# Expert slots of a mixture-of-experts layer: small slots with the rows as the stationary operand, two low halves on GpSimd, and a later place for one weight half in big slots

## The chip, the cores and the metric

The kernel runs on one core of one Trainium2 chip. The metric is the device time in microseconds of one execution of the whole program. TensorE (PE) multiplies, VectorE (DVE), ScalarE (ACT) and GpSimd (POOL) do the elementwise work, and SyncE (SP) issues the loads and stores of this stage. The engines run side by side and wait for each other only at semaphores.

## The reference, cut to what matters

Two layers act on 4096 rows of 256 numbers. The part that the change touches is the feed-forward half of the second layer, in which each row goes to one of eight experts:

```python
gate_logits = jnp.einsum('bsd,ed->bse', x, gate_w) + gate_b + expert_bias
top_idx = jnp.argmax(gate_logits, axis=-1)
for e in range(8):
    mask = (top_idx == e)[..., None].astype(x.dtype)
    h = jax.nn.relu(jnp.einsum('bsd,df->bsf', x, w1[e]) + b1[e])   # 256 -> 1024
    y = jnp.einsum('bsf,fd->bsd', h, w2[e]) + b2[e]                # 1024 -> 256
    out = out + mask * y
```

All of it is in float32. Beside it the same rows go through four gated linear scans (the attention half of that layer), and before it stands a first layer with an attention of chunks of 32 rows and sixteen small experts.

## The kernel before, in words

**Stages.** The first half of the time is the first layer. Then the scans of the second layer begin: eight groups of 512 rows. After the first four groups the experts run, and then the other four groups and the sum of everything. This order is written out by hand for every engine; there is no planner.

**Slots.** The rows are sorted by expert (scattered to DRAM) and handled in 23 slots, one after the other. A big slot has 256 rows (two blocks), a small one 128 (one block). A round is big, big, small (k = 0, 1, 2); there are seven full rounds (`ROUND`, index r) and two big slots at the end. Each slot belongs to one expert, whose number is read from a table (`expert(n)`, a register load on SyncE), and each slot loads that expert's weights afresh: w1 (256 x 1024) and w2 (1024 x 256), 1 MB each, in halves of 512 KB.

**Split products.** To keep the accuracy of float32, each operand is split in a high part (rounded to float32r) and a low part (the rest), and each product is three matmuls: high by high, high by low, low by high (`mm3`). So for every half of a weight ScalarE writes the high part (`w1_half`, line 1405, and `w2_half`, line 1412) and VectorE subtracts to get the low part (lines 1702 and 1713), both 128 x 1024. The raw halves are single buffers: SyncE loads a half for a later slot (`raw1_half`, line 1195, `raw2_half`, line 1202) as soon as the low part of the present one is formed.

**One slot n on TensorE.** Layer 1 computes the hidden values transposed: the weights are stationary, the rows are the moving operand, 256 columns wide in a big slot and 128 in a small one; 8 blocks of 128 hidden units, 6 matmuls each, 48 in all (lines 372 to 374). They fill four PSUM banks, the quarters q = 0 to 3. Then the rows of the next slot are transposed (`rows_T`, line 1326). Layer 2 multiplies the hidden values (stationary) by w2, 256 columns wide: 48 matmuls in a big slot, 24 in a small one (lines 1360 to 1362).

**One slot on ScalarE.** The second half of w2's high part (it waits until the slot before has ended layer 2); then for each quarter a ReLU with bias (two instructions, line 1430) and a rounding (line 1436). After the second quarter stands the first half of w1 for slot n + 1, after the fourth the high part of the next rows (line 1417), w1's second half and w2's first half for slot n + 1.

**One slot on VectorE.** The same order: the result of the slot before out of PSUM with its bias (line 1728), w2's second half, the four low parts of the hidden values (line 1719) with w1's first half after the second, then the next rows' low part (line 1707), w1's second half and w2's first half.

**One slot on SyncE.** One queue, in order, and each wait holds up all behind it:

```python
store_y(...)                          # slot n - 1, waits for its result
load_b2(n)
raw2_half(n + 1, 1, e)                # waits for the low part w2, half 1, of slot n
load_rows(r, k + 2)                   # waits for the transposes of slot n + 1
load_b1(n + 1, e)                     # waits for the ReLUs of slot n
raw1_half(n + 2, 0, e)                # waits for the low part w1, half 0, of slot n + 1
raw1_half(n + 2, 1, e)
raw2_half(n + 2, 0, e)
```

**GpSimd** does nothing in the slots. The functions that the diff touches, and what calls them:

## Time and profile before

| | |
|---|---|
| median of 3 runs | 1065.47 us (1065.38 to 1067.77) |
| the profiled execution | 1066.7 us |
| its span, first to last instruction | 1064.7 us |
| mean granted TensorE clock | 0.994 |
| busy: TensorE, VectorE, ScalarE, GpSimd | 98%, 73%, 60%, 35% |
| expert slots | about 667 to 918 us of the span |

The profile is one execution. Its own time stands beside its span; the few microseconds around the span are not in the trace. Times in the rows are microseconds from the span's start. A row of a timeline gives the start, the length, the engine, the line, the operation, what it writes and reads with its shapes, and in brackets how long the engine was idle before and what ended that. Matmuls overlap in the pipeline, so what one costs is the distance from start to start and not its length.

### The profile page before, as it was taken

The numbers are of one execution on the slowest core, as the hardware profiler recorded it, in microseconds if no ns is written. First come the engines' busy times: TensorE is split into PE (matmuls) and PEld (weight loads), VectorE is DVE, ScalarE is ACT, GpSimd is POOL, SyncE is SP. The second block draws the span as 40 slices with busy tenths as digits, with TensorE's granted clock in tenths as the row PEclk, the third lists the DMA queues.
The fourth block names the chain that finished last, engine by engine and source line by source line (L and its number), as shares of the span: only waits on it lengthen the run. The fifth ranks groups of instructions, "written<-read, shape, count | busy, mean of one in ns | idle before, by whom it ended". The sixth has DMA issues, their size and how long they took to land. (4 is left out here: it accounts for less than half of the span.)

```text
span 1064.7 us, 20417 instructions
## 1 busy us (share of the span) xinstructions
PE 1039.9 (98%) x6692; PEld 933.5 (88%) x6692; DVE 773.6 (73%) x1281; ACT 638.7 (60%) x1152; POOL 373.1 (35%) x309
## 2 busy tenths in 40 slices
PE   6999999999999999999999999899999999999996
PEld 5998888989889898888877888899999999988885
DVE  5865657556575565758689889887778787588888
ACT  4554444444444444445574656789888989566664
POOL 3344443444434344453471782000000000164451
PEclk9999999999999999999999999999999999999998
DMA  5215111010111101203236366588787877332224
GB/s 178 73 56 198 41 40 59 26 73 0 39 59 39 59 0 59 79 1 139 66 115 257 109 221 233 160 250 268 241 262 241 268 247 247 126 119 99 108 70 138
DMA packets 72683, 134.73 MB, mean 127 GB/s; under 512 B 10048, under 2 KB 42688, under 8 KB 71616
## 3 DMA queue, kind: packets, MB, share of 16 engines
q1 hardware_dynamic: 63280, 120.65, 33.8%
q0 software_dynamic: 3072, 8.39, 2.4%
q10 hardware_dynamic: 6288, 5.16, 1.4%
q8 instruction: 22, 0.36, 0.1%
q14 instruction: 21, 0.17, 0.1%
HBM read 98.72 MB, written 35.45 MB: 126 GB/s over the span
## 5 line engine op out<-in xcount | busy, mean ns | idle before, releaser
L712 POOL TENSOR_TENSOR acc<-acc,ytmp 128x512 f32<-128x512 f32 x120 | 156.7, 1306 | 248.2 <-ACT ytmp L800 234.8
L1387 ACT ACTIVATE act_o<-ps,scan_bias 128x512 f32<-128x512 f32 x192 | 129.8, 688 | 103.5 <-PE ps L374 86.9
L865 DVE SCALAR_TENSOR_TENSOR hT_l<-ps,hT_h 128x512 fp32r<-128x512 f32 x128 | 87.8, 686 | 117.0 <-ACT hT_h L763 116.9
L800 ACT ACTIVATE ytmp<-ps,sel 128x256 f32<-128x256 f32 x256 | 107.6, 472 | 100.5 <-PE ps L1015 99.9
L372 PE MATMUL ps<-x1T,WB_h 128*128 128x512 f32 (+1 forms) x384 | 152.7, 398 | 2.3 <-DMA x1T<-xT_d 2.3
L374 PE MATMUL ps<-x1T,WB_l 128*128 128x512 f32 (+1 forms) x384 | 151.4, 394 | 0.0
L373 PE MATMUL ps<-x1T,WB_h 128*128 128x512 f32 (+1 forms) x384 | 150.1, 391 | 0.0
L1013 PE MATMUL ps<-vals_h,hT_h 128*128 128x256 f32 x512 | 145.2, 284 | 0.4 <-DVE hT_l L865 0.4
L1014 PE MATMUL ps<-vals_l,hT_h 128*128 128x256 f32 x512 | 143.6, 281 | 0.0
L1015 PE MATMUL ps<-vals_h,hT_l 128*128 128x256 f32 x512 | 143.4, 280 | 0.0
L763 ACT ACTIVATE hT_h<-ps 128x512 fp32r<-128x512 f32 x128 | 76.5, 598 | 99.6 <-PE ps L374 99.5
L1529 POOL DMA_INDIRECT y_b<-y_d,pos_i x20 | 25.3, 1267 | 296.9 <-DMA y_d<-y_sb 275.3
L901 DVE SCALAR_TENSOR_TENSOR acc<-ps,sel,acc 128x256 f32<-128x256 f32 x240 | 104.0, 474 | 3.0 <-PE ps L1015 2.9
L372 PE MATMUL ps<-xT_h,keys_h 128*128 128x512 f32 x256 | 104.6, 408 | 1.1 <-DVE xT_l L413 1.1
L1013 PEld LDWEIGHTS ps<-vals_h,hT_h 128*128 128x128 f32 x512 | 96.3, 188 | 8.8 <-issue 3.0
L1656 DVE TENSOR_TENSOR_SCAN h_b<-a_b,hstate,xs_b 128x512 f32<-128x512 f32 x64 | 91.7, 1433 | 16.9 <-ACT a_b L1392 11.5
L372 PE MATMUL ps<-sT_h,w_h 128*128 128x256 f32 (+1 forms) x368 | 102.4, 278 | 0.5 <-DVE w_l L1702 0.5
L374 PE MATMUL ps<-sT_h,w_l 128*128 128x256 f32 (+1 forms) x368 | 102.6, 279 | 0.0
L373 PE MATMUL ps<-sT_l,w_h 128*128 128x256 f32 (+1 forms) x368 | 102.6, 279 | 0.0
L374 PE MATMUL ps<-xT_h,keys_l 128*128 128x512 f32 x256 | 101.1, 395 | 0.0
L373 PE MATMUL ps<-xT_l,keys_h 128*128 128x512 f32 x256 | 101.0, 395 | 0.0
L1014 PEld LDWEIGHTS ps<-vals_l,hT_h 128*128 128x128 f32 x512 | 96.2, 188 | 4.4
(220 smaller groups left out, 2647.1 us busy)
## 6 DMA issues: line engine op xcount, KB each, us to landing
raw<-w SPq DMA_DIRECT2D x92, 512.0 KB, 4.9
x1T<-xT_d SPq DMA_DIRECT2D x16, 512.0 KB
comb_b<-comb_d SPq DMA_DIRECT2D x8, 1024.0 KB
xs_d<-zeros ACTq DMA_DIRECT2D x1, 4992.0 KB, 18.8
x_in<-x SPq DMA_DIRECT2D x8, 512.0 KB, 3.8
x_d<-x SPq DMA_DIRECT2D x8, 512.0 KB, 4.2
xn_d<-xn SPq DMA_DIRECT2D x8, 512.0 KB, 2.6
xT_d<-nT_h SPq DMA_DIRECT2D x8, 512.0 KB, 2.6
```

The lines of the kernel that those rows point to most:

```text
L372: pe.matmul(dst, wh, xh, start=start, stop=False)
L373: pe.matmul(dst, wh, xl, start=False, stop=False)
L374: return pe.matmul(dst, wl, xh, start=False, stop=stop)
L712: pool.tensor_tensor(dst[:, 2:4, :], acc[:, 2:4, :], ytmp[:, k % 2, :, :], ALU.add).then_inc(acc23, 1)
L800: act.activation(ytmp[:, k % 2, j - 2, :], yb(k, j), ACT.Copy, scale=sel[:, j, k:k + 1]).then_inc(y_23, 1)
L865: dve.scalar_tensor_tensor(out=hT_l[:, k % 2, :], in0=ps[:, k % 2, :], scalar=0.0, in1=hT_h[:, k % 2, :].bitcast(F32), op0=ALU.max, op1=AL ...
L901: dve.scalar_tensor_tensor(out=dst[:, j, :], in0=yb(k, j), scalar=sel[:, j, k:k + 1], in1=acc[:, j, :], op0=ALU.mult, op1=ALU.add).then_in ...
L1013: pe.matmul(yb(k, j), hT_h[:, k % 2, s], vals_h[:, k, :], start=True, stop=False)
L1014: pe.matmul(yb(k, j), hT_h[:, k % 2, s], vals_l[:, k, :], start=False, stop=False)
L1015: last_mm = pe.matmul(yb(k, j), hT_l[:, k % 2, s], vals_h[:, k, :], start=False, stop=True)
L1387: act.activation(act_o[:, i % 2, w, :], ps[:, 3 * (i % 2) + w, :], func, bias=scan_bias[:, w, i:i + 1]).then_inc(act_g, 1)
L1656: dve.tensor_tensor_scan(h_b[:, i % 2, :], a_b[:, i % 2, :], xs_b[:, i % 2, :], hstate[:, i:i + 1], ALU.mult, ALU.add).then_inc(scan_ok, 1)
```

## The change

**Small slots, TensorE.** Layer 1 has the rows stationary and the weights moving: two halves of the hidden units, 512 columns each, 6 matmuls each, into PSUM banks 0 and 1. The hidden values then stand with rows on the partitions and must be turned: eight transposes of 128 x 128 in three pieces (2, 2 and 4 of them), the transposes of the next rows between the second piece and the third.

**Small slots, the others.** VectorE adds the bias of each half (`rows_biased`, out of PSUM); the bias now lies along the free dimension, so a new buffer `b1b` of 128 x 1024 is loaded by one 512 KB broadcast instead of `b1c` (4 KB). ScalarE does one ReLU to each turned piece, which writes the high part at once (`relu_rows`), and VectorE one operation for its low part (`low_rows`). ScalarE's order is w2's second half, w1's first half of the next slot, the three ReLUs, then as before.

**GpSimd** forms two low halves in each small slot: w2's second half of this slot and w1's first half of the next. It counts on semaphores of its own.

**Big slots.** w2's second half stands after w1's first half, behind the second quarter, on ScalarE and on VectorE, and no longer ahead of the first. TensorE's wait for the ReLUs of the slot before is gone. SyncE's order stays; its waits follow the low parts, wherever they are formed (`w1_last`, `w2_last`).

```diff
+    PIECES = ((2, 0, 1), (3, 1, 1), (0, 2, 2))
...
-            def raw2_half(n, h, e):
-                if not zero(n):
-                    wait_alone(sp, w2_lo, 2 * (n - 1) + h + 1)
+            def raw2_half(r, k, h, e):
+                if not (zero(r) and k == 0):
+                    wait_alone(sp, *w2_last(r, k, h))
...
-            def load_b1(n, e):
-                if not zero(n):
-                    wait_alone(sp, t_ok, FJ * n)
+            def load_b1(r, k, e):
+                if small(k):
+                    if not zero(smalls(r, k)):
+                        wait_alone(sp, row_out, 2 * smalls(r, k))
+                    sp.dma_start(b1b[:], a["b1r"][bass.ds(e, 1)].to_broadcast((P, F1))).then_inc(b1b_in, 16)
+                    return
+                if not zero(bigs(r, k)):
+                    wait_alone(sp, t_ok, FJ * bigs(r, k))
...
+            def first_layer_rows(r, k):
+
+                for h in (0, 1):
+                    pe.wait_ge(*w1_low(r, k, h))
+                    f = slice(h * HALF1, (h + 1) * HALF1)
+                    for c in range(DC):
+                        last_mm = mm3(pe, ps[:, h, :], sT_h[:, c, 0:P], sT_l[:, c, 0:P], w1_h[:, c, f], w1_l[:, c, f],
+                                      c == 0, c == DC - 1)
+                    last_mm.then_inc(l1_full, 2)
+
+            def turn_rows(r, pieces):
+
+                for bank, q, nq in pieces:
+                    pe.wait_ge(row_out, 2 * r + 1 + q // 2)
+                    for j in range(2 * nq):
+                        f = slice((2 * q + j) * P, (2 * q + j + 1) * P)
+                        last_mm = pe.transpose(ps[:, bank, j * P:(j + 1) * P], h_rows[:, f], ident[:])
+                    last_mm.then_inc(rT_full, nq)
...
-                for q in range(FJ // 2):
-                    if not zero(n):
-                        pe.wait_ge(t_ok, FJ * (n - 1) + 2 * q + 2)
-                    elif q == 3:
+                if small(k):
+                    first_layer_rows(r, k)
+                    turn_rows(r, PIECES[0:2])
+                    rows_T(r, k + 1)
+                    turn_rows(r, PIECES[2:3])
+                for q in range(0 if small(k) else FJ // 2):
+                    if zero(n) and q == 3:
...
+            def relu_rows(r, bank, q, nq):
+                act.wait_ge(rT_full, FJ // 2 * r + q + nq)
+                act.activation(eT_h[:, 2 * q:2 * (q + nq), 0:P],
+                               ps[:, bank, 0:2 * nq * P].rearrange("p (j t) -> p j t", t=P), ACT.Relu).then_inc(e_hi, nq)
+
             def slot(r, k):
                 n, (_, st) = ROUND * r + k, blocks(r, k)
-                w2_half(n, 1)
+                if small(k):
+                    w2_half(n, 1)
+                    w1_half(n + 1, 0)
+                    for bank, q, nq in PIECES:
+                        relu_rows(r, bank, q, nq)
+                    rows_hi(r, k + 1)
+                    w1_half(n + 1, 1)
+                    w2_half(n + 1, 0)
...
                 for q in range(FJ // 2):
-                    relu(n, q, st * P)
-                    round_e(n, q, st * P)
-                    if q == 1 and left(r, k) > 0:
-                        w1_half(n + 1, 0)
+                    relu(n, bigs(r, k), q, st * P)
+                    round_e(bigs(r, k), q, st * P)
+                    if q == 1:
+                        if left(r, k) > 0:
+                            w1_half(n + 1, 0)
+                        w2_half(n, 1)
...
+            for r in range(N_SMALL):
+                n = ROUND * r + ST
+                j, f = slice(HALF2, FJ), slice(0, HALF1)
+                pool.wait_ge(w2_hi, 2 * n + 2)
+                pool.tensor_tensor(w2_l[:, j, :], raw2[:, j, :], w2_h[:, j, :].bitcast(F32), ALU.subtract).then_inc(w2_lo_p, 1)
+                pool.wait_ge(w1_hi, 2 * (n + 1) + 1)
+                pool.tensor_tensor(w1_l[:, :, f], raw1[:, :, f], w1_h[:, :, f].bitcast(F32), ALU.subtract).then_inc(w1_lo_p, 1)
...
+            def rows_biased(r, k, h):
+                n = ROUND * r + k
+                dve.wait_ge(l1_full, FJ // 2 * n + 2 * (h + 1))
+                if h == 0:
+                    dve.wait_ge(b1b_in, 16 * (smalls(r, k) + 1))
+                f = slice(h * HALF1, (h + 1) * HALF1)
+                dve.tensor_tensor(h_rows[:, f], ps[:, h, :], b1b[:, f], ALU.add).then_inc(row_out, 1)
+
+            def low_rows(r, k, bank, q, nq):
+                n = ROUND * r + k
+                dve.wait_ge(e_hi, FJ // 2 * n + q + nq)
+                j = slice(2 * q, 2 * (q + nq))
+                dve.scalar_tensor_tensor(out=eT_l[:, j, 0:P],
+                                         in0=ps[:, bank, 0:2 * nq * P].rearrange("p (j t) -> p j t", t=P),
+                                         scalar=0.0, in1=eT_h[:, j, 0:P].bitcast(F32), op0=ALU.max,
+                                         op1=ALU.subtract).then_inc(e_ok, nq)
...
-                w2_half(n, 1)
+                if small(k):
+                    rows_biased(r, k, 0)
+                    rows_biased(r, k, 1)
+                    for bank, q, nq in PIECES:
+                        low_rows(r, k, bank, q, nq)
+                    rows_lo(r, k + 1)
+                    w1_half(n + 1, 1)
+                    w2_half(n + 1, 0)
```

## Rows read from the trace of the kernel before

**Rows 1.** The page, part 1: busy time, share, count.
```profile
PE 1039.9 (98%) x6692; PEld 933.5 (88%) x6692; DVE 773.6 (73%) x1281; ACT 638.7 (60%) x1152; POOL 373.1 (35%) x309
```

**Rows 2.** Windows: one small slot, then its two big ones; busy by engine.
```profile
core 0: us, PE busy (x) PEld busy (x) DVE busy (x) ACT busy (x) POOL busy (x), PEclk, DMA share, GB/s
727.56:736.14 8.58, 8.58 (x78) 8.58 (x77) 6.13 (x10) 7.76 (x17) 0.00 (x0) 1.00 0.91 289
736.14:747.87 11.73, 11.73 (x103) 11.73 (x102) 9.92 (x12) 10.47 (x18) 0.00 (x0) 1.00 0.77 243
747.87:759.40 11.53, 11.53 (x101) 11.53 (x100) 8.62 (x11) 9.77 (x17) 0.00 (x0) 1.00 0.71 233
```

**Rows 3.** TensorE's timeline, small slot: start, length, line, operation.
```profile
...
727.56 0.22 PE L372 MATMUL ps<-sT_h,w_h 128*128 128x128 f32 x1
...
732.87 0.62 PE L1326 MATMUL ps<-ident,rows 128*128 128x128 f32 x4
...
736.14 0.28 PE L372 MATMUL ps<-sT_h,w_h 128*128 128x256 f32 x1
```

**Rows 4.** TensorE's timeline, earlier stage: 512-column matmuls, then eight transposes.
```profile
557.78 0.39 PE L373 MATMUL ps<-x1T,WB_h 128*128 128x512 f32 x1
...
560.07 0.40 PE L374 MATMUL ps<-x1T,WB_l 128*128 128x512 f32 x1
...
590.07 1.03 PE L1289 MATMUL ps<-ident,accT 128*128 128x128 f32 x8
590.87 0.47 PE L372 MATMUL ps<-x1T,WB_h 128*128 128x512 f32 x1
```

**Rows 5.** Timeline of ScalarE and of VectorE, a big slot.
```profile
749.49 0.84 ACT L1430 ACTIVATE t<-ps,b1c 128x256 f32<-128x256 f32 x2 [0.35 <-PE ps L374]
...
752.31 1.05 ACT L1405 ACTIVATE w_h<-raw 128x1024 fp32r<-128x1024 f32 x1
753.27 0.82 ACT L1430 ACTIVATE t<-ps,b1c 128x256 f32<-128x256 f32 x2
...
749.16 1.23 DVE L1713 TENSOR_TENSOR w_l<-raw,w_h 128x1024 fp32r<-128x1024 f32 x1 [0.22 <-ACT w_h L1412]
...
753.39 1.23 DVE L1702 TENSOR_TENSOR w_l<-raw,w_h 128x1024 fp32r<-128x1024 f32 x1 [0.26 <-ACT w_h L1405]
```

**Rows 6.** Timeline of ScalarE and of VectorE: tiles read from PSUM.
```profile
734.25 0.58 ACT L1417 ACTIVATE sT_h<-ps 128x512 fp32r<-128x512 f32 x1
...
756.05 0.37 ACT L1417 ACTIVATE sT_h<-ps 128x256 fp32r<-128x256 f32 x1
...
734.87 0.69 DVE L1707 TENSOR_TENSOR sT_l<-ps,sT_h 128x512 fp32r<-128x512 f32 x1
```

**Rows 7.** Timeline of SyncE's queue: when each load is issued.
```profile
755.72 0.33 SPq L1215 DMA_DIRECT2D b1c<-b  x1
757.05 2.37 SPq L1195 DMA_DIRECT2D raw<-w  x2
...
765.55 0.38 SPq L1210 DMA_DIRECT2D rows<-xs_d  x1
766.26 0.33 SPq L1215 DMA_DIRECT2D b1c<-b  x1
```

**Rows 8.** The tile raw (both weights' halves) in the slots: issue to landing.
```profile
DMA to landing us min/median/max: 4.1/4.9/5.1
```

**Rows 9.** The view of one line of GpSimd: durations least/median/most in ns, first and last start.
```profile
L719 POOL TENSOR_TENSOR xT<-xT_h,xT_l x8: 2400/2410/2851, 23.4 to 468.7; 128x1024 f32<-128x1024 f32 x8
```

**Rows 10.** GpSimd's timeline where VectorE works on two SBUF tiles.
```profile
537.47 2.21 POOL L527 TENSOR_TENSOR WB_l<-stage_b,WB_h 128x512 fp32r<-128x512 f32 x1
```

**Rows 11.** TensorE's timeline after an idle stretch, earlier stage.
```profile
562.77 0.50 PE L372 MATMUL ps<-x1T,WB_h 128*128 128x512 f32 x1 [2.30 <-DMA x1T<-xT_d]
...
564.43 0.63 PE L372 MATMUL ps<-x1T,WB_h 128*128 128x512 f32 x1
...
567.42 0.42 PE L373 MATMUL ps<-x1T,WB_h 128*128 128x512 f32 x1
```

More of the change, by code:

```diff
@@ L194, in build @@
     b2b = rc("b2b", [P, D], F32)
+    b1b = rc("b1b", [P, F1], F32)
+    h_rows = t32[:, 0:FJ // 2, :].rearrange("p j t -> p (j t)")
     w1_h = rc("w1_h", [P, DC, F1], F32R)
@@ L579, in build @@
     scat = [sem(f"scat{b}") for b in range(XN_RING)]
-    b1_in, b2_in, rows_in = (sem(n) for n in ("b1_in", "b2_in", "rows_in"))
+    b1_in, b1b_in, b2_in, rows_in = (sem(n) for n in ("b1_in", "b1b_in", "b2_in", "rows_in"))
+    row_out, rT_full = sem("row_out"), sem("rT_full")
+    w1_lo_p, w2_lo_p = sem("w1_lo_p"), sem("w2_lo_p")
     r1_in, r2_in = [sem(f"r1_in{h}") for h in (0, 1)], [sem(f"r2_in{h}") for h in (0, 1)]
@@ L605, in blocks, with bigs, smalls, small @@
         return (4 * r + ST * k, ST) if k < ST else (T // P + r, 1)
+    def bigs(r, k):
+        return ST * (r + k // ROUND) + min(k % ROUND, ST)
+    def smalls(r, k):
+        return r + k // ROUND
+    def small(k):
+        return k % ROUND == ST
+    def w1_low(r, k, h):
+        r, k = r + k // ROUND, k % ROUND
+        if k == 0 and h == 0 and not zero(r):
+            return w1_lo_p, r
+        return w1_lo, (2 * ROUND - 1) * r + 2 * k + h + 1
+    def w2_low(r, k, h):
+        r, k = r + k // ROUND, k % ROUND
+        if small(k) and h == 1:
+            return w2_lo_p, r + 1
+        return w2_lo, (2 * ROUND - 1) * r + 2 * k + h + 1
+    def w1_last(r, k, h):
+        r, k = r + k // ROUND, k % ROUND
+        return w1_low(r, k - 1, h) if k else (w1_lo, (2 * ROUND - 1) * r + h)
+    def w2_last(r, k, h):
+        r, k = r + k // ROUND, k % ROUND
+        if k:
+            return w2_low(r, k - 1, h)
+        return (w2_lo_p, r) if h else (w2_lo, (2 * ROUND - 1) * r)
+    PIECES = ((2, 0, 1), (3, 1, 1), (0, 2, 2))
     def every_slot(slot, eng):
@@ L1196, in raw1_half @@
                              a["w1"][bass.ds(e, 1), h].rearrange("a p c f -> p (a c) f")).then_inc(r1_in[h], 16)
-            def raw2_half(n, h, e):
-                if not zero(n):
-                    wait_alone(sp, w2_lo, 2 * (n - 1) + h + 1)
+            def raw2_half(r, k, h, e):
+                if not (zero(r) and k == 0):
+                    wait_alone(sp, *w2_last(r, k, h))
                 j = slice(h * HALF2, (h + 1) * HALF2)
@@ L1347, in slot @@
                     last_mm.then_inc(l1_full, 1)
-                if left(r, k) > 0:
+                if left(r, k) > 0 and not small(k):
                     rows_T(r, k + 1)
@@ L1449, in slot @@
                     w2_half(n + 1, 0)
-                if zero(r) and k == 2:
-                    mixture_sigmoids(act, mix2, 2)
                 if left(r, k) == 1:
@@ L1744, in slot @@
                     rows_out(*((r, k - 1) if k else (r - 1, ROUND - 1)))
-                w2_half(n, 1)
+                if small(k):
[6 more added lines that the diff above has]
+                    w2_half(n + 1, 0)
+                    if zero(r):
+                        mixture_pieces(k)
+                    return
                 for q in range(FJ // 2):
                     low_e(n, q, st * P)
-                    if q == 1 and left(r, k) > 0:
-                        w1_half(n + 1, 0)
+                    if q == 1:
+                        if left(r, k) > 0:
+                            w1_half(n + 1, 0)
+                        w2_half(n, 1)
                 if left(r, k) > 0:
```

47 lines of the change are left out of this document (25 added, 22 removed).

## The prediction

> **What bounds the kernel now.** I read the page's busy shares first, then the windows of one round, then the timelines of the engines in it. TensorE is busy for 98% of the span [rows 1]. The change lies in the 23 expert slots. One small slot and its two big ones last 8.58, 11.73 and 11.53 us, TensorE is busy in all of it at the full clock, and no other engine is [rows 2]. So this stage is TensorE's: what it saves there counts, as long as nobody makes it wait. The reader is to see two more things in the windows: ScalarE is busy 7.76 of the 8.58 us of a small slot, and the DMA share there is already 0.91, at 289 GB/s [rows 2].
>
> All sums are made against the profiled execution, 1066.7 us (span 1064.7). The median of the three runs is 1065.47, 1.2 us lower; I take 1.2 off at the end. I count 0.3%, 3.2 us, as about what a measurement of this kernel tells from no change.
>
> **TensorE's own sum, per small slot.** Layer 1 with the weights stationary is 48 matmuls of 128 columns, 727.56 to 732.87: 5.31 us, 0.111 each [rows 3]. The rest, 732.87 to 736.14, is four transposes of the next rows and 24 matmuls of 256 columns: 3.27 us [rows 3]. With rows stationary, layer 1 is 12 matmuls of 512 columns. Ten such starts took 557.78 to 560.07, 0.229 each [rows 4]: 12 cost 2.75 us. Eight transposes of 128x128 are added, and eight took 590.07 to 590.87, 0.80 us [rows 4]. So 5.31 goes, 3.55 comes: 1.76 less per small slot, 12.3 for seven. With no wait at all the slot is 6.82 us and the profiled time 1054.4.
>
> **The chain inside the small slot.** Layer 1's sum now passes VectorE (bias), TensorE (transposes), ScalarE (ReLU) and VectorE (low part) before layer 2. Count from the slot's start. Layer 1 ends at 2.75; a handoff to another engine costs about 0.2 (in a big slot 12 of 96 matmuls, 11.3 us by rows 2, end at 1.42, and ScalarE's ReLU starts at 749.49, 1.62 after 747.87 [rows 2, 5]). The bias on 128x512 is a PSUM read of 0.69 [rows 6], to 3.6; the last four transposes end at about 4.1; ReLU on 128x512, 0.58, and the low part, 0.69 [rows 6], end at about 5.6. Layer 2's first half runs until then, and its second half, 1.44, ends at 7.0 to 7.1. So the chain's floor is 7.1, not 6.82: 1.5 less than now, 10.4 us in all. ScalarE and VectorE lose work in this slot (eight ReLUs and four roundings become three ReLUs; two low parts go to GpSimd), so their busy time is no bound.
>
> **GpSimd's two low halves.** A two-input operation on 128x1024 took 2.41 us there [rows 9] against VectorE's 1.23 [rows 5]. The first starts when ScalarE has rounded the second half of weight 2, near 2.4 (below), and ends at 4.8; layer 2 wants it at about 5.6 or later. The second follows ScalarE's rounding of the next slot's weight 1, first half. Both are covered, at a cost of nothing, if GpSimd isn't slowed; a rival has the price of the lost cover.
>
> **The moved step, and SyncE's queue.** This is where I part from the full gain. In a big slot ScalarE rounded the second half of weight 2 first, and VectorE's low part ended at 749.16 + 1.23 = 750.39, 2.52 into the slot [rows 5]. Now both come after the second quarter and after weight 1's first half. ScalarE takes that half at 752.31, 4.44 in, 0.96 each [rows 5], so the moved rounding is 5.40 to 6.4. VectorE takes the weight 1 part at 753.39, 5.52 in, 1.23 long [rows 5], and ends the moved part near 7.95 (twice 1.23, less a little overlap). For layer 2 of the same slot that is in time: its last 24 matmuls begin 2.8 before the end, at 8.7. The later two ReLU quarters are 0.96 later; the third's low part ends near 8.5, against 8.7: a cover of only 0.2, which I cost at nothing (losing it costs what it overshoots, in 16 slots).
>
> But SyncE's queue is in order, and its next load, raw2's second half for the next slot, waits for that low part. Behind it stand the rows load, the new b1b load, then raw1's first half for the slot after. Issues without a wait stand 0.71 apart, 1.33 where an expert number is read first [rows 7]. From 7.95: rows 8.66, b1b 9.37, raw1 first half 10.70. Before, that raw1 load was issued at 757.05, 9.18 in [rows 2, 7]. It is 1.5 later. And ahead of it in 2.75 us go 512 + 256 + 512 KB, where b1c was a few KB.
>
> Who waits? In the small slot ScalarE's order is: second half of weight 2, then the first half of weight 1 that this load brings, and only then the three ReLUs. Its wait holds back the ReLUs, and so layer 2. With L from issue to landing, and the big slot 11.53 long [rows 2], it lands L - 0.83 into the small slot. Then 0.96 rounding, 0.42 ReLU of a 128x256 piece (0.37 [rows 6] and a bit), about 0.45 for its low part (0.69 [rows 6], scaled by ScalarE's 0.37/0.58), and 24 matmuls, 2.87. The slot is L + 3.9. It equals today's 8.58 at L = 4.7. GpSimd's second part ends 2.4 after the rounding, before the slot does.
>
> L is 4.1 least, 4.9 median, 5.1 most in this stage today [rows 8]. Lower bound 4.1: slot 8.0, 4.1 us saved in all. Upper bound: 289 GB/s at share 0.91 is 318 GB/s flat out [rows 2], so 1.31 MB needs 4.1 us where 2.75 have passed; 4.9 + 1.35 = 6.25, slot 10.15, 11 us lost. The nearest row is the 5.1 of a half queued behind others, so I take 5.2: slot 9.1, +0.5 in each of seven, +3.6. b1b, issued 1.33 earlier, holds the bias back to about 3 and TensorE's turning with it, but that wait lies under ScalarE's and adds nothing. Sum: 1066.7 + 3.6 - 1.2 = 1069.1.
>
> The Trainium skill's page DMA: Bandwidth & Descriptors, section Anatomy of one DMA — SWDGE (gpsimd) path, fits 2.0 us plus bytes over 436 GB/s to each transfer of that path; by it a half of 512 KB would take an estimated 3.2 us, the wait would go, and the second rival below would come true. The trace disagrees: no half landed under 4.1.
>
> **Other edits.** ScalarE's first work in a big slot is gone, which gives nothing since the ReLU waits for TensorE at 1.62 anyway [rows 5]. TensorE's wait for the ReLUs of the slot before never bound. The 512 KB b1b load seven times is counted above. Everything ahead of the slots and after them is unchanged.
>
> **Rivals.**
> 1. Forecast: raw1's first half is late, L 4.1 to 6.25, 1061 to 1076, likeliest 1069. For it: the queue order and rows 7 and 8. Against: only half a microsecond from balance.
> 2. Faster: the load is in time (L under 3.8, or SyncE issues earlier than I reckon, with ScalarE free by 3.5 of the slot). Then b1b is next: landing near 3, bias 3.7 and 4.4, four transposes, ReLU and low part to 6.1, slot 7.1 to 7.6, 1054 to 1060. For it: ScalarE has over 1.7 us less work. It decides below L = 4.2.
> 3. The clock. After 2.30 idle seven 512-column matmuls took 564.43 to 567.42, 0.427 each instead of 0.229 [rows 4, 11]: the 1.2 GHz level instead of 2.4, at 1.4 us more. My small slot has 2.2 us of idle, in two pieces. If a fall comes each time, seven times 1.4 more: 1079. One or two falls are inside the forecast.
> 4. GpSimd is slowed. Its 128x512 operation took 2.21 beside VectorE's two-input work [rows 10] instead of 1.2 (half of 2.41). At 4.4 for a half, weight 1's low part comes 9.6 into the slot, past its end of 9.1: 4 us more, 1073. Against: VectorE's work in that stretch reads PSUM. Beside this stands the Trainium skill, SBUF — State Buffer, section Who interferes with whom: a VectorE instruction with two SBUF inputs and a GpSimd one that reads SBUF exclude each other, one with a PSUM input does not. The 2.21 agrees; by the rule only the two weight parts at the slot's end can collide.
>
> **Chances.** Rival 1 0.63 (slower 0.31, same 0.24, faster 0.08), rival 2 0.18 (0.16 faster, 0.02 same), rival 3 0.11, rival 4 0.08, both slower. Slower 0.50, same 0.26, faster 0.24. The likeliest gives 1069.0; its own range is 1062 to 1075. For 8 in 10 over all I take 1058.5 to 1075.5: it leaves out the best of rival 2 and most of rival 3.
>
> **What would show it.** Right: L1405's successor waiting 2 us and more for the raw DMA in small slots; TensorE idle before layer 2 there; small slots near 9; SyncE waiting 3 us for VectorE's moved part; 512-column matmuls 0.229 apart; big slots still 11.5 to 11.7. Wrong: small slots of 7 to 8 us without a DMA wait; clock below 1.00 in most rounds; TensorE waiting for GpSimd's part; big slots longer.

## The result and the profile after

The changed kernel takes 1084.61 us (median of four runs, 1084.39 to 1086.36) where the kernel before takes 1065.97 (four runs, 1065.38 to 1067.77): the ratio is 1.0177, 95% interval 1.0165 to 1.0189. It is 18.6 us slower. The forecast was 3.6 us slower, 1069.1, with 1075.5 as the upper end of its range. The profiled execution of the changed kernel took 1084.73, with a span of 1082.9.

The page shows TensorE with less work (1034.8 us busy instead of 1039.9) and a smaller share, 96% where [rows 1] have 98%:

```profile
PE 1034.8 (96%) x6496; PEld 920.3 (85%) x6496; DVE 765.4 (71%) x1274; ACT 617.9 (57%) x1089; POOL 407.2 (38%) x323
```

I measured each slot from its first layer-1 matmul to that of the next slot. The whole loss lies there: the 23 slots take 269.1 us instead of 251.0, 18.1 more. In order, a semicolon after each round, the changed kernel's slots are 17.42, 11.55, 12.70; 11.78, 11.64, 10.88; 11.72, 11.63, 10.42; 11.73, 11.63, 10.50; 11.72, 11.63, 10.31; 11.73, 11.62, 10.96; 11.72, 11.63, 11.05; 11.75, 11.36. Before they were 16.91, 11.50, 8.58, and then 11.73, 11.50, 8.58 six times. So the seven small slots cost 16.8 us more, the second big slots 0.8, and the first slot 0.5. Windows over one round (two big slots, then the small one), to lay beside [rows 2]:

```profile
core 0: us, PE busy (x) PEld busy (x) DVE busy (x) ACT busy (x) POOL busy (x), PEclk, DMA share, GB/s
743.44:755.16 11.72, 11.72 (x103) 11.72 (x101) 8.08 (x11) 9.79 (x17) 0.00 (x0) 1.00 0.64 213
755.16:766.79 11.63, 11.63 (x100) 11.57 (x99) 8.59 (x11) 9.68 (x18) 0.00 (x0) 1.00 0.73 232
766.79:777.21 10.42, 7.39 (x50) 6.27 (x49) 6.43 (x11) 5.67 (x8) 4.77 (x2) 1.00 0.92 318
```

In the small slot TensorE is busy 7.39 of 10.42 us; in [rows 2] it was busy in all of 8.58. Its own timeline says where it stands idle (compare [rows 3]):

```profile
766.79 0.39 PE L374 MATMUL ps<-w_h,sT_h 128*128 128x512 f32 x1
...
769.36 0.39 PE L376 MATMUL ps<-w_h,sT_l 128*128 128x512 f32 x1
771.69 0.66 PE L1395 MATMUL ps<-ident,t 128*128 128x128 f32 x4 [1.94 <-DVE t L1821]
772.18 0.60 PE L1375 MATMUL ps<-ident,rows 128*128 128x128 f32 x4
772.62 0.60 PE L1395 MATMUL ps<-ident,t 128*128 128x128 f32 x4
774.30 0.39 PE L1431 MATMUL ps<-w_h,eT_h 128*128 128x256 f32 x1 [1.09 <-DVE eT_l L1827]
...
777.21 0.28 PE L374 MATMUL ps<-sT_h,w_h 128*128 128x256 f32 x1
```

Layer 1 is as short as reckoned: twelve matmuls from 766.79 to 769.36 and one pitch, 0.233 each, 2.8 us. Then come two waits: 1.94 us for the bias add (L1821) before the hidden values are turned (L1395, the transposes), and 1.09 for the ReLU's low part (L1827) before layer 2 (L1431). ScalarE shows what stands behind the second:

```profile
766.99 1.07 ACT L1483 ACTIVATE w_h<-raw 128x1024 fp32r<-128x1024 f32 x1 [0.33 <-PE ps L1433]
772.46 1.06 ACT L1476 ACTIVATE w_h<-raw 128x1024 fp32r<-128x1024 f32 x1 [4.40 <-DMA raw<-w]
773.43 1.12 ACT L1511 ACTIVATE eT_h<-ps 128x256 fp32r<-128x256 f32 x3
```

It waits 4.40 us for raw1's first half, with the three ReLUs queued behind. The view of waits over the stage counts it (what waited, for whom, us in total, times, longest):

```profile
ACT w_h L1476 <- DMA raw<-w: 30.5, 7, 4.6
...
PE ps L1395 <- DVE t L1821: 16.1, 7, 3.9
DVE t L1821 <- DMA b1b<-b1r: 14.0, 6, 2.6
```

SyncE's queue in the same round, to lay beside [rows 7]:

```profile
763.44 0.34 SPq L1246 DMA_DIRECT2D raw<-w  x1
764.27 0.38 SPq L1254 DMA_DIRECT2D rows<-xs_d  x1
764.91 0.33 SPq L1260 DMA_DIRECT2D b1b<-b1r  x1
766.23 1.53 SPq L1239 DMA_DIRECT2D raw<-w  x2
```

raw1's first half is issued 11.07 us into the big slot (766.23 less 755.16) and ScalarE starts on it 6.23 later. I call this time L. In the six later rounds it is 6.46, 6.23, 6.26, 6.11, 6.24 and 6.37. The prediction's L ends at the landing, for which it took 5.2; the traces give no landing for this half in the changed kernel, and where they give one (x13, the later rounds) ScalarE starts 0.1 after it.

### The profile page after: what moved, and what is told of

Read it like the earlier page. It is cut to its first block and busy times, and to the rows that moved or that the text cites. A ratio compares the mean times of both kernels' runs of the same rounds, so it can differ in the third digit from the quotient of the medians.

```text
span 1082.9 us, 19855 instructions
## 1 busy us (share of the span) xinstructions
PE 1034.8 (96%) x6496; PEld 920.3 (85%) x6496; DVE 765.4 (71%) x1274; ACT 617.9 (57%) x1089; POOL 407.2 (38%) x323
## 5 line engine op out<-in xcount | busy, mean ns | idle before, releaser
L1749 DVE TENSOR_TENSOR_SCAN h_b<-a_b,hstate,xs_b 128x512 f32<-128x512 f32 x64 | 92.2, 1440 | 16.8 <-ACT a_b L1463 11.4
L1431 PE MATMUL ps<-w_h,eT_h 128*128 128x256 f32 x312 | 90.9, 291 | 6.6 <-DVE eT_l L1827 4.5
L1059 PEld LDWEIGHTS ps<-vals_h,hT_l 128*128 128x128 f32 x512 | 96.8, 189 | 0.0
L1645 POOL TENSOR_TENSOR w_l<-raw,w_h 128x1024 fp32r<-128x1024 f32 x7 | 16.6, 2374 | 210.1 <-ACT w_h L1483 210.1
L1432 PE MATMUL ps<-w_l,eT_h 128*128 128x256 f32 x312 | 87.4, 280 | 0.0
```

What stands on the lines that cost most here:

```text
L1059: last_mm = pe.matmul(yb(k, j), hT_l[:, k % 2, s], vals_h[:, k, :], start=False, stop=True)
L1431: pe.matmul(dst, eT_h[:, j, t], w2_h[:, j, :], start=j == 0, stop=False)
L1749: dve.tensor_tensor_scan(h_b[:, i % 2, :], a_b[:, i % 2, :], xs_b[:, i % 2, :], hstate[:, i:i + 1], ALU.mult, ALU.add).then_inc(scan_ok, 1)
```

## The experiments

Theories. Q: the moved rounding holds SyncE's queue, and that is the loss. B: the new bias load, 512 KB in the queue ahead of raw1's first half, is slow itself and delays what stands behind it. Against them: ScalarE's order in the small slot, GpSimd's part, the clock, and theory M, the first round's gate pieces on VectorE (`mixture_pieces`: small operations on 128x32 and less that rank the rows' gate values; they run only in the first round). Every ratio is to the kernel before, run on the same chip beside it. A slot's time is read from one profiled execution of each kernel.

| kernel | edit | median us | ratio, 95% interval |
|---|---|---|---|
| x1 | changed, move undone | 1065.7 | 0.9993 (0.9978 to 1.0009) |
| x2 | before, move alone | 1074.1 | 1.0075 (1.0058 to 1.0092) |
| x3 | changed, b1b loaded once | 1077.5 | 1.0098 (1.0081 to 1.0115) |
| x4 | changed, raw1's half issued first | 1078.9 | 1.0134 (1.0089 to 1.0178) |
| x5 | x1, gate pieces after the small slot | 1067.0 | 0.9998 (0.9984 to 1.0013) |
| x6 | x1, other queue order | 1065.1 | 0.9989 (0.9973 to 1.0005) |
| x7 | x5 and x6 | 1063.6 | 0.9965 (0.9952 to 0.9978) |
| x8 | changed, other queue order, move kept | 1072.5 | 1.0052 (1.0034 to 1.0070) |
| x9 | x6, gate pieces in the first slot | 1061.8 | 0.9949 (0.9933 to 0.9966) |
| x10 | x1, GpSimd's halves on VectorE | 1067.4 | 1.0005 (0.9994 to 1.0016) |
| x11 | changed, ReLUs first | 1086.4 | 1.0181 (1.0155 to 1.0208) |
| x12 | before, GpSimd's halves alone | 1073.1 | 1.0058 (1.0037 to 1.0080) |
| x13 | changed, biases stored 128 times | 1081.8 | 1.0147 (1.0125 to 1.0169) |
| x14 | changed, b1b into one partition | 1079.2 | 1.0111 (1.0092 to 1.0129) |

### x1: the move undone

```diff
+                w2_half(n, 1)
                 for q in range(FJ // 2):
 ...
-                    if q == 1:
-                        if left(r, k) > 0:
-                            w1_half(n + 1, 0)
-                        w2_half(n, 1)
+                    if q == 1 and left(r, k) > 0:
+                        w1_half(n + 1, 0)
```

The same on ScalarE and on VectorE, in big slots only.

> The changed kernel, with the second half of weight 2 again first in big slots. Theory Q, the moved half holds back SyncE's queue and that is the whole loss: raw1's first half is issued 1.5 us earlier and lands in 5.2, small slots fall from 10.7 to 8.2 or less, time about 1067. Theory B, the 512 KB bias load is itself slow and holds up raw1's first half behind it in the queue: the half is issued 1.3 us earlier but still takes 6.2 us to land, small slots 9.3 to 9.4, time 1074 to 1076. If neither the queue nor the load sets the small slot (the new chain through VectorE and TensorE costs it), nothing changes: 1084.

Measured 1065.7, near Q's 1067 and 9 us under B's 1074 to 1076: all of the loss goes. In the profile a big slot starts at 755.15, the small one behind it at 766.65. SyncE's queue, then ScalarE:

```profile
762.15 0.33 SPq L1260 DMA_DIRECT2D b1b<-b1r  x1
763.47 3.35 SPq L1239 DMA_DIRECT2D raw<-w  x2
```

```profile
769.50 1.07 ACT L1476 ACTIVATE w_h<-raw 128x1024 fp32r<-128x1024 f32 x1 [1.59 <-DMA raw<-w]
```

raw1's first half is issued 8.32 us in, 2.75 earlier than in the changed kernel; I had reckoned with 1.3. The kernel before issued it at 9.18 because b1c ahead of it waits for the slot's last ReLUs [rows 7]; b1b waits for nothing recent. L is still 6.03. With the half 2.75 earlier ScalarE waits only 1.59, and after the first round small slots are 7.53 to 8.02. So Q names the edit that costs, while B's slow load is there too and is now nearly hidden. The profile is of one of the two executions of ten that took 1071.5 (the others took 1063.5 to 1067.1), and its first round is long: 18.30 in its first big slot and 14.35 in its small one, at a granted clock of 0.81 and 0.76.

### x2: the move alone, in the kernel before

```diff
-                w2_half(n, 1)
+                if small(k):
+                    w2_half(n, 1)
                 for q in range(FJ // 2):
 ...
                     if q == 1 and left(r, k) > 0:
                         w1_half(n + 1, 0)
+                    if q == 1 and not small(k):
+                        w2_half(n, 1)
```

> The kernel before, with only the move of weight 2's second half in big slots. Theory Q at full strength: raw1's first half is 1.5 us later and small slots grow by about that, 1076. Theory B: behind it there is no bias load of 512 KB, it lands in 5.1, near 4.2 into the small slot, and ScalarE, which does two ReLU quarters ahead of it, comes to it at about 3.5: small slots 0 to 0.7 longer, 1066 to 1071.

Measured 1074.1, 8 us more than before, over B's 1066 to 1071 and under Q's 1076. The mechanism is neither as I wrote it: small slots stay at 8.58 to 8.84, and it is the big slot behind them that grows, from 11.73 to between 12.11 and 12.99. ScalarE there:

```profile
773.47 0.84 ACT L1434 ACTIVATE t<-ps,b1c 128x256 f32<-128x256 f32 x2 [2.21 <-DMA b1c<-b]
```

Its first ReLU waits for b1c, a load of 4 KB that stands behind the halves and the rows. The waits of this stage hold that wait six times, 10.1 us; the kernel before has none. SyncE's row for that load:

```profile
768.98 0.33 SPq L1219 DMA_DIRECT2D b1c<-b  x1
```

It is issued 6.90 into the small slot (which starts at 762.08), as before (766.26 less 759.37, 6.89 [rows 7]). So it isn't issued late but lands late: ScalarE starts on it 4.5 after its issue, where before 3.4 (766.26 to 769.65) was enough. What differs ahead of it is the queue. The move keeps SyncE still until 8 to 9 us into the big slot and then lets five loads (raw2's second half, the rows, and the three halves for the slot after) go in a bunch. That b1c pays for this bunch fits the rows; no run separates it.

### x3, x14, x13: what b1b costs the load behind it

```diff
# x3: only the first round's load is left, and VectorE waits for that one
+                if small(k) and not zero(smalls(r, k)):
+                    return
                 if small(k):
-                    if not zero(smalls(r, k)):
-                        wait_alone(sp, row_out, 2 * smalls(r, k))
...
# x14: later loads go to one partition, 4 KB
-                    sp.dma_start(b1b[:], a["b1r"][bass.ds(e, 1)].to_broadcast((P, F1)))...
+                    p = P if zero(smalls(r, k)) else 1
+                    sp.dma_start(b1b[0:p, :], a["b1r"][bass.ds(e, 1)].to_broadcast((p, F1)))...
# x13: 512 KB as before, but 128 different rows
-                    sp.dma_start(b1b[:], a["b1r"][bass.ds(e, 1)].to_broadcast((P, F1)))...
+                    sp.dma_start(b1b[:], a["b1r"][bass.ds(e, 1)].rearrange("a p f -> (a p) f"))...
...
-        "b1r": c(i["L1_ffn_b1"]),
+        "b1r": c(np.repeat(i["L1_ffn_b1"][:, None, :], P, axis=1)),
```

> The changed kernel with the bias load b1b only ahead of the first small slot; the later small slots use that one's bias, so their rows are those of another expert's bias. Theory B: raw1's first half is issued 0.65 us earlier and lands in 5.2 instead of 6.2 to 6.5, small slots about 8.7 to 8.9, time 1071 to 1073. Theory Q alone: only the 0.65 of the issue comes back, small slots about 10.0, time 1080.

> The changed kernel, b1b loaded whole ahead of the first small slot and later into one partition only (4 KB; the other 127 keep the first one's bias). Issue, order and wait stay, the 512 KB go. If b1b's transfer is what costs (R or its bytes): raw1's first half lands 4.1 after its issue at 11.0, small slots 8.3 to 9, and as in x3 the slot behind them waits for b1c: 1076 to 1079. If the issue and its place cost: 1084.

> The changed kernel with the biases stored 128 times over in the chip's memory, so that b1b is still 512 KB to 128 partitions, but no two of them read the same row. In the changed kernel raw1's first half lands 6.2 after its issue behind b1b, in x3, with no b1b, 4.1, and while b1b moves the DMA engines carry 189 GB/s instead of 400. Theory R, the one row read 128 times is slow: b1b then moves at 400 GB/s, 1.3 us, raw1's first half lands in 5.2 to 5.4, small slots 9.7 to 9.9, time 1077 to 1080. Theory P, it is the place or the bytes of any such load: 6.2 stays, and 1084.

L of the six later rounds, from SyncE's issue to ScalarE's start:

| kernel | L of each round | mean |
|---|---|---|
| changed | 6.46 6.23 6.26 6.11 6.24 6.37 | 6.3 |
| x13, 128 rows | 5.29 5.96 5.57 5.22 5.59 6.17 | 5.6 |
| x3, no b1b | 4.71 4.06 3.88 5.05 4.82 3.91 | 4.4 |
| x14, 4 KB | 5.13 3.66 3.84 4.82 3.98 3.78 | 4.2 |

One pair of rows for L in x3 (issue, then ScalarE's start):

```profile
765.70 2.12 SPq L1239 DMA_DIRECT2D raw<-w  x2
```

```profile
769.76 1.07 ACT L1476 ACTIVATE w_h<-raw 128x1024 fp32r<-128x1024 f32 x1 [1.61 <-DMA raw<-w]
```

So b1b's issue and its place cost nothing measurable in L (x14 against x3; they cost 0.6 to 0.7 by making raw1's issue later, 11.1 to 11.2 into the slot against 10.5). 512 KB of different rows cost 1.4 us of L (x13 against x14), and that the 128 partitions read one row costs 0.65 more (6.28 less 5.63). b1b's own landing shows the cost of the one row directly, 0.9; first the changed kernel, then x13:

```profile
DMA to landing us min/median/max: 5.5/6.0/6.2
```

```profile
DMA to landing us min/median/max: 5.0/5.1/5.3
```

Windows over the stretch in which b1b moves and, for the changed kernel, the one behind it agree; first the changed kernel, then x13:

```profile
766.50:770.00 3.50, 3.25 (x16) 2.36 (x15) 2.20 (x3) 1.23 (x2) 1.86 (x1) 1.00 0.76 189
770.00:773.00 3.00, 1.31 (x12) 1.29 (x12) 1.29 (x2) 0.54 (x1) 0.52 (x1) 1.00 1.03 400
```

```profile
766.50:770.00 3.50, 3.33 (x17) 2.43 (x15) 2.28 (x3) 1.31 (x2) 1.79 (x1) 1.00 0.92 304
```

With one row the DMA engines carry 189 GB/s, with 128 rows 304. Theory B holds in this size. But the gains in time are small, 3 us in x13, 5 in x14, 7 in x3, and the times miss what I expected: x13's 1081.8 lies between R's 1077 to 1080 and P's 1084, and x3's 1077.5 is over B's 1071 to 1073. In x3 and x14 a part is given back. x3's small slots fall to between 7.53 and 8.68 after the first round, and the big slots behind them, 11.73 in the kernel before, take 12.25 to 14.13, where ScalarE waits for b1c as in x2:

```profile
778.76 0.47 ACT L1501 ACTIVATE t<-ps,b1c 128x256 f32<-128x256 f32 x1 [2.53 <-DMA b1c<-b]
```

### x4 and x8: another order in SyncE's queue, the move kept

```diff
# x4, in SyncE's slot; and not again further down where k == 1
+                if k == 1 and left(r, k) > 1:
+                    raw1_half(r, k + 2, 0, expert(n + 2))
                 if left(r, k) > 0:
                     e = expert(n + 1)
# x8 has this, and x6's edit
```

> The changed kernel; in the second big slot of a round SyncE issues raw1's first half ahead of raw2's second half, the rows and the bias, about 7 us into the slot instead of 11. Both theories: ScalarE's wait for it goes. Theory B: then the bias load, issued near 10.5 and landing after 5.5 to 6.2, sets the small slot: the bias add starts 4.5 to 5 in, small slots 8.6 to 9.1, time 1070 to 1073. Theory Q: nothing else is late, small slots 7.1 to 7.6, time 1059 to 1063. If the clock falls in most small slots, 1.4 more in each.

> The changed kernel with the move kept, and SyncE's queue in another order: raw1's first half ahead of raw2's second half in the second big slot, b1b at the end of the first, b1c first in the small one. Theory Q: the move costs only by what stands behind its low part in SyncE's queue, so that most of the 19 us come back: 1064 to 1068 (the first round's 4 us stay). Rival: raw2's own second half, now issued 8.3 us into the slot and behind 512 KB more, is late for the small slot's layer 2: small slots 9 to 10, 1074 to 1080.

x4 issues raw1's first half 7.1 us into the slot, and ScalarE no longer waits for it. But small slots come down only to between 8.55 and 10.66 after the first round, and the time is 1078.9: as B said, the bias load is next (VectorE waits for b1b seven times, 12.9 us in all), and raw2's second half, now behind raw1's, is late as well (ScalarE waits for it seven times, 13.3 us in all). It came out above the range of either theory. x8 brings b1b and b1c forward too and ends at 1072.5, between Q's 1064 to 1068 and the rival's 1074 to 1080; its small slots are 8.18 to 8.83 after the first round. There the moved half itself is late: its load can only be issued once VectorE has freed the buffer, 8.5 us into the slot (762.42 less 753.90), and in the small slot ScalarE waits for it:

```profile
767.98 1.07 ACT L1493 ACTIVATE w_h<-raw 128x1024 fp32r<-128x1024 f32 x1 [2.57 <-DMA raw<-w]
```

So the move costs in more ways than by what stands behind it; the orders that I tried get back at most 12 of the 19 us.

### x11: the ReLUs first

```diff
                     w2_half(n, 1)
-                    w1_half(n + 1, 0)
                     for bank, q, nq in PIECES:
                         relu_rows(r, bank, q, nq)
+                    w1_half(n + 1, 0)
```

> The changed kernel with ScalarE's three ReLUs of a small slot ahead of weight 1's first half. If ScalarE's order was the loss (the wait for raw1 held up the ReLUs): TensorE's turning ends at 5.3 to 5.9 into the slot, set by the bias load, layer 2 at 9.2, the slot 1.4 shorter, 1074 to 1076. Rival: weight 1's first half itself is late. It lands 6.2 in, is rounded by 7.3, and GpSimd's part takes 2.4 more: the next slot can't start before 9.9 to 10.2 in, so small slots come down by 0.3 to 0.7 only: 1079 to 1082.

1086.4, no gain. ScalarE's order alone isn't the loss. What the ReLUs gain, weight 1's first half loses: it is rounded after them, GpSimd's 2.4 us follow, and TensorE waits for that part at the start of the next slot (the waits: TensorE for GpSimd's L1647, seven times, 6.9 us). That is the rival, with less left over than I put on it: the later small slots come down by 0.28 in the mean, not 0.3 to 0.7, the first one grows from 12.70 to 13.89, and the time was 1086.4 instead of 1079 to 1082.

### x5, x7, x9: the first round's gate operations

```diff
# x5: the pieces of the second big slot, at the end of the small one
                     if zero(r):
-                        mixture_pieces(k)
+                        mixture_pieces(1)
+                        mixture_pieces(2)
...
-                if zero(r):
-                    mixture_pieces(k)
+                if zero(r) and k == 0:
+                    mixture_pieces(0)
# x9: the same pieces at the end of the first big slot
-                if zero(r):
-                    mixture_pieces(k)
+                if zero(r) and k == 0:
+                    mixture_pieces(0)
+                    mixture_pieces(1)
```

> The kernel with the move undone; of the first round's small gate operations on VectorE (the mixture pieces) those that stood at the end of the second big slot are done at the end of the small one. Theory M: in the first round they hold VectorE until 4.9 us into the small slot (one of 128x16 took 2.40 us while GpSimd's half ran), and the bias add and TensorE's turning wait for it: the first small slot falls from 14.35 (12.70 in the changed kernel) to 8 to 9, a clock fall in it goes, and the time falls by 3 to 5 us, to 1061 or 1062. Rival: the first round is long for the start of the stage itself, and nothing changes: 1065 to 1066.

> x5 and x6 together. If their gains add: 1056 to 1058, small slots 7.1 to 7.4, the first included. The floor reckoned with the prediction's chain (7.1 per small slot) is 1055. If GpSimd's second half or the clock is next, 1060 to 1063.

> The kernel of x6 (move undone, SyncE's queue in the other order), and the first round's small gate operations that stood at the end of the second big slot now at the end of the first. Theory M in the form that x5 and x7 left (done after the small slot they hold the slot behind it): ahead of GpSimd's halves and two slots before the bias add they hold nobody. The first small slot falls from x6's 12.84 to 7.5, nothing after it grows: 4.5 to 5 us under x6, 1060 to 1061. If some other engine or the clock is what makes the first round long, it stays at 1064 to 1065.

In the changed kernel the first small slot is 12.70 and not 10.3 to 11.1. VectorE's timeline there:

```profile
697.65 0.17 DVE L477 TENSOR_TENSOR cmp<-logits 128x16 f32<-128x16 f32 x1
697.86 2.40 DVE L479 TENSOR_TENSOR rank<-rank,cmp 128x16 f32<-128x16 f32 x1
700.29 0.17 DVE L477 TENSOR_TENSOR cmp<-logits 128x8 f32<-128x8 f32 x1
...
701.92 0.69 DVE L1838 TENSOR_TENSOR y_sb<-ps,b2b 128x512 f32<-128x512 f32 x1
702.53 1.28 DVE L1821 TENSOR_TENSOR t<-ps,b1b 128x512 f32<-128x512 f32 x2
```

and GpSimd's beside it:

```profile
697.85 2.37 POOL L1645 TENSOR_TENSOR w_l<-raw,w_h 128x1024 fp32r<-128x1024 f32 x1 [50.84 <-ACT w_h L1483]
```

An operation of 0.18 us lasts 2.40, until GpSimd's ends. The gate pieces behind it are done only at 701.92, the bias add starts at 702.53, and TensorE stands idle for 3.87 us:

```profile
703.26 1.12 PE L1395 MATMUL ps<-ident,t 128*128 128x128 f32 x4 [3.87 <-DVE t L1821]
```

Four transposes then take 1.12 instead of 0.66: the granted clock from 703.26 to 704.40 is 0.50, the 1.2 GHz level. x5 shortens this slot to 7.63, as M said, but the slot behind it grows to 13.52, since ScalarE's two sigmoids now wait for the gate pieces (3.44 us, in front of the rounding and the ReLUs); the total stays (0.9998), and my expectation of 1061 was wrong. x7 has the same, 7.47 and 13.66, and at 1063.6 misses the 1056 to 1058 of added gains. x9 does the pieces where GpSimd has nothing to do: first small slot 7.47, next 11.73, but the second big slot 13.11 for 11.50. x10 (below) bears on GpSimd's share: without its halves the first small slot is 10.59, against 14.35 in x1 (granted clock 0.84 against 0.76). x9 is the fastest kernel here, 0.51% under the kernel before (interval 0.34 to 0.67). It took 1061.8, and I expected 1060 to 1061.

### x6: the order of the queue, the move undone

```diff
                     e = expert(n + 1)
+                    if small(k):
+                        load_b1(r, k + 1, e)
                     raw2_half(r, k + 1, 1, e)
 ...
-                    load_b1(r, k + 1, e)
+                    if not small(k):
+                        load_b1(r, k + 1, e)
 ...
                     raw2_half(r, k + 2, 0, e)
+                    if k == 0:
+                        load_b1b(r, 2)
```

load_b1b is the load of b1b, taken out of load_b1, with its wait.

> The kernel with the move undone; the bias load b1b is issued last in the first big slot of the round instead of ahead of raw1's first half in the second, and in the small slot b1c is loaded ahead of raw2's second half. Theory B (what stands behind b1b and in a bunch is late): ScalarE's wait for raw1's first half in small slots, 1.6 of 7.6 to 8.0 us, goes and with it 0.4 to 0.9 of each small slot; the first big slots' 12.2 to 12.3 in later rounds fall back to 11.7; together 4 to 7 us, 1059 to 1062. Rival: b1b's 512 KB have only moved into another bunch, and 0 to 2 us come back: 1064 to 1066.

1065.1, ratio 0.9989: the rival's 1064 to 1066, not B's 1059 to 1062. The slots are what B asked for: small ones 7.52 to 7.54 after the first, big ones 11.72 and 11.50. The profiled stage is 2.6 us shorter than before (248.3), and 5.3 us of its first small slot (12.84) are left in it; x9 takes them out and loses 1.6 in the slot ahead. Windows over one round of x9:

```profile
735.66:747.38 11.72, 11.72 (x103) 11.72 (x101) 8.76 (x12) 9.84 (x17) 0.00 (x0) 1.00 0.75 239
747.38:758.88 11.50, 11.50 (x100) 11.50 (x99) 9.08 (x12) 9.75 (x17) 0.00 (x0) 1.00 0.91 308
758.88:766.42 7.54, 7.33 (x51) 6.39 (x49) 5.45 (x9) 5.72 (x8) 4.74 (x2) 1.00 0.87 278
```

7.54 is the small slot's chain with rows stationary and no load on it, 1.04 less than 8.58. ScalarE still waits 0.95 for raw1's first half in this slot of x9; in five of x6's seven rounds it doesn't wait for that load at all, and the slot is the same 7.52 to 7.54.

### x10 and x12: GpSimd's part

```diff
# x10 on VectorE, small slots; GpSimd's loop is left out
+                    w2_half(n, 1)
                     rows_biased(r, k, 0)
                     rows_biased(r, k, 1)
                     for bank, q, nq in PIECES:
                         low_rows(r, k, bank, q, nq)
+                    w1_half(n + 1, 0)
# x12: the kernel before with GpSimd's loop; on VectorE
-                w2_half(n, 1)
+                if not small(k):
+                    w2_half(n, 1)
 ...
-                    if q == 1 and left(r, k) > 0:
+                    if q == 1 and left(r, k) > 0 and not small(k):
```

> The kernel with the move undone, and both of GpSimd's low halves done by VectorE again (128x1024 in 1.23 us instead of 2.39). If GpSimd's part is needed: VectorE's own work in a small slot is then 0.42 + four times 1.23 + 0.69 + 0.69 + 0.76 + 0.69 + 0.68, 8.8 us, more than the 7.5 to 8.0 of the slot: small slots 8.5 to 9.3, 1069 to 1073. If VectorE's idle time hides it, or GpSimd's hold on VectorE was a loss of its own: 1063 to 1067.

> The kernel before with GpSimd's two halves alone: no move, weights stationary. Expected: small slots stay at 8.58, since TensorE has 8.58 of work there; the first round's gate operations are held 2 us by GpSimd with no effect. 1065 to 1067. Rival: raw2's second half is freed 1.2 us later in each small slot and b1c behind it comes late for the next slot's first ReLU: up to 1 us in each of seven, 1067 to 1073.

x10: small slots are 7.99 to 8.07 after the first, against 7.53 to 8.02 in x1; the time, 1.0005, doesn't differ from x1's by what can be told. GpSimd's part gains little with rows stationary. x12: in the kernel before it costs 0.58%, small slots 9.25 instead of 8.58. Expected was nothing (1065 to 1067), or b1c late (up to 1073); it is neither, but VectorE's low parts of the ReLU. Groups of these by shape, in the same stretch of the stage, the kernel before and then x12 (count, busy us, mean ns):

```profile
L1719 DVE TENSOR_TENSOR eT_l<-t,eT_h 128x256 fp32r<-128x256 f32 x24 | 10.2, 424 | 8.1 <-ACT eT_h L1436 7.7
```

```profile
L1757 DVE TENSOR_TENSOR eT_l<-t,eT_h 128x256 fp32r<-128x256 f32 x24 | 23.1, 997 | 18.2 <-ACT eT_h L1467 18.2
```

424 ns become 997 in the mean. The mean mixes two kinds: in each small slot two of the four low parts stay at 0.42, and the two that start while one of GpSimd's halves runs last 1.39 and 1.75, until 0.3 after it ends (763.03 to 764.42, GpSimd's to 764.13). Both inputs of this operation lie in SBUF. With rows stationary the same step reads PSUM and SBUF, and it isn't slowed (changed kernel):

```profile
L1827 DVE SCALAR_TENSOR_TENSOR eT_l<-ps,eT_h 128x256 fp32r<-128x256 f32 x13 | 5.0, 420 | 9.5 <-ACT eT_h L1511 9.5
```

The Trainium skill, SBUF — State Buffer, section Who interferes with whom, says that a VectorE instruction with two SBUF inputs contends with a GpSimd one that reads SBUF, and one with at most one, outside of the modes that use both ports, does not. The two groups in kernels with GpSimd's halves, x12's 997 and the changed kernel's 420, agree with it. So does x11, where VectorE's low part of weight 1's second half comes to stand beside GpSimd's and lasts 2.07 to 2.09 us in each small slot instead of 1.23.

## Why the prediction was wrong, point by point

The direction and the place were right: slower, in the small slots, by ScalarE's wait for raw1's first half. The size was not: 3.6 us forecast, 18.1 in the profiled stage. The step of the sum that failed is L, the time that this load takes: 5.2 taken, 6.3 measured, 6.5 of the missing 14.5 us. The rest is spread over the steps below.

- **TensorE's sum.** Right within 0.2. Layer 1 took 2.8 us (2.75 reckoned), and each set of four transposes 0.44 to 0.49 (0.40 reckoned).
- **The chain's floor, 7.1.** A little low: 7.54 where no load is on the chain (x6, x9).
- **GpSimd's halves covered, at nothing.** Right for GpSimd: they took 2.37 and 2.39. Rival 4, GpSimd slowed, didn't come. The hold falls on VectorE, and the forecast didn't price that side; in the changed kernel it strikes in the first round only, in x11 and x12 in every one.
- **The moved step.** VectorE's low part ended 7.99 into the slot (763.15 less 755.16); 7.95 was reckoned. The issue of raw1's first half was 11.07 instead of 10.70: 0.3 lies between the low part's end and SyncE's next issue, and the sum left it out. The big slot was 11.63 instead of 11.53. Together 0.27 of this small slot, 0.32 in the mean of six.
- **L, the failed step.** "The nearest row is the 5.1 of a half queued behind others, so I take 5.2". L was 6.3 in the mean, at the upper bound of 6.25 that stood beside it; this is 1.08 of each later small slot, 6.5 us in six. The row of 5.1 was a half without b1b's 512 KB ahead of it, and x13 and x14 show that these bytes cost 1.4. On top comes the one row read by 128 partitions, 0.65, which no row of the kernel before shows. That the bound of 6.25 came so near is partly luck: it is 4.9 and 1.35 for the bytes, where the runs show 4.2 (x14), 1.43 and 0.65.
- **Rows 8, read too narrowly.** The 4.1, 4.9 and 5.1 were called those of this stage, but the view is of 727 to 880 only, and all its fifteen landings are of raw1's second halves; the trace has none of a first half, the load in question. The stage's other landings of such halves reach from 3.8 (its first slot) to 6.0 (at 705.47). So "no half landed under 4.1" doesn't hold for the stage, and the fit that stood beside it is for loads issued by GpSimd, while these are SyncE's.
- **The rest of the chain.** From ScalarE's start to the slot's end it was 4.75 to 4.77 against 4.70, but 5.24 and 5.26 in the two rounds with a fall of the clock.
- **Sum of these.** A slot of 10.42: 11.07 less 11.63, plus 6.23, plus 4.75. Over six rounds the mean is 10.69, 1.6 over the 9.1 forecast, 9.5 us in all: 1.08 of L, 0.32 of the moved step, and 0.2 behind it, most of it from the clock.
- **The first round.** 3.6 us over 9.1 in its small slot and 0.5 in its first big one: not foreseen. The 0.5 isn't shown to be the change's: x13, with the same code there, took 16.91, as the kernel before. For the 3.6: the change makes the bias add a step of VectorE on the path, so that what VectorE did there before at no cost (the gate pieces, end of the second big slot) is now waited for, and GpSimd holds it there. The prediction named what is queued on SyncE and ScalarE, and not on VectorE.
- **The cover of 0.2 in the big slots.** Lost: second big slots are 0.12 to 0.14 longer, 0.8 us in all.
- **Rival 3, the clock.** Came in the first small slot and in two of the six later ones, not each time; granted clock in those two, windows of the changed kernel:

```profile
868.09:879.05 10.96, 8.89 (x50) 7.71 (x49) 6.39 (x10) 5.75 (x8) 4.76 (x2) 0.84 0.90 309
902.40:913.45 11.05, 8.90 (x50) 7.85 (x49) 6.20 (x10) 5.65 (x8) 4.75 (x2) 0.85 0.92 306
```

  A fall costs 0.5 (the rest of the chain, above); the forecast had 1.4. The second round's 10.88 is at full clock, and its load was late. Both falls came at the first of the two idle pieces, one in it and one within 0.4 us behind it. Two rows, the second round's at full clock and the sixth's, whose transposes are slower:

```profile
737.79 0.65 PE L1395 MATMUL ps<-ident,t 128*128 128x128 f32 x4 [2.27 <-DVE t L1821]
```

```profile
873.12 0.92 PE L1395 MATMUL ps<-ident,t 128*128 128x128 f32 x4 [2.07 <-DVE t L1821]
```

- **Rival 2, the load in time.** Not in this kernel. With the load in time (x4), b1b was next, as it said, but at 8.6 to 10.7, not at 7.1 to 7.6: b1b lands 5.0 to 6.0 after its issue there, and raw2's second half is late too.

1.6 times six, 3.6, 0.5 and 0.8 make 14.5, what the stage took over the forecast.

What stays open: the 7 us by which x8, with the move kept, stands above x6. ScalarE's wait for raw2's second half is seen in it, but I didn't separate it from the bunching of the other loads. Of the 1.6 that x9 loses in its second big slot only the place is shown. And the length of the first big slot goes from 16.39 to 18.34 over the profiles, with a clock of 0.81 in x1's; why is not shown.

## What to carry to other kernels

Before a step is moved later on the engines that free a buffer, write down everything that the queue of loads holds behind the wait for that buffer: here one rounding, moved back within slots whose own layer 2 wants it late, held five loads of other buffers, and undoing it gave back all 19 us. For the landing time of a load take the bytes that are issued just ahead of it on its queue, not the median of other loads, and look which loads that median is made of. When a change puts an engine on the critical path, list what that engine did in the new place before, in every round, the first one too.

## What was unexpected of the hardware

- One 4 KB row read into 128 partitions (512 KB) moves slower than 128 different rows: it lands 6.0 us after its issue against 5.1, the DMA engines carry 189 GB/s in the stretch around it against 304, and the next load is ready 0.65 us later.
- A VectorE operation with two SBUF inputs that starts while a GpSimd one runs was held until that ended, however short it was: 0.18 us became 2.40 beside GpSimd's 2.37, 0.42 became 1.39 and 1.75 (x12), 1.23 became 2.07 to 2.09 (x11).
- TensorE's granted clock fell to the 1.2 GHz level in 3.87 us of idle, in 2.15 and right behind 2.07 between busy stretches, but not at 2.27 nor at three of 1.88 to 1.94 (the first idle piece of the changed kernel's seven small slots).
